# Two chained cross-attentions: where ScalarE copies a product's part and where VectorE takes the product out

## The reference

```python
# L0, per batch: x is 100 x 128, ctx is 1444 x 128
normed = x * rsqrt(mean(x**2) + 1e-6) * norm_w
q, k, v = heads(normed @ wq), heads(ctx @ wk), heads(ctx @ wv)
attn = softmax(einsum('bhqd,bhkd->bhqk', q, k))
x1 = x + merge(einsum('bhqk,bhkd->bhqd', attn, v)) @ wo
# L1
w = softmax(einsum('brd,bfd->brf', x1, ctx))
out = x1 + einsum('brf,bfd->brd', w, ctx)
```

## Time and profile before

| | us |
|---|---|
| median of 3 runs | 591.34 (590.78 to 592.22) |
| profiled execution | 590.37 |
| its span, first to last instruction | 588.6 |
| TensorE busy | 567.8 |
| VectorE busy | 456.6 |
| ScalarE busy | 392.8 |
| GpSimd busy | 457.4 |

### The profile page before, as it was taken

One profiled execution on the slowest core, in us unless ns is written; L12 is line 12 of the kernel. 1 busy time (PEld: TensorE's weight loads), 2 busy tenths in 40 slices (PEclk: granted clock), 3 DMA queues, 4 the chain that ended last, 5 costly groups with the idle time before them and its releaser, 6 DMA issues.

```text
span 588.6 us, 10834 instructions
## 1 busy us (share of the span) xinstructions
PE 567.8 (96%) x3748; PEld 513.4 (87%) x3748; DVE 456.6 (78%) x642; ACT 392.8 (67%) x515; POOL 457.4 (78%) x532
## 2 busy tenths in 40 slices
PE   7799999899999999999999999999999999999997
PEld 7678889799999899898989899998999888988885
DVE  4667789779886898868987798868987798868505
ACT  5567676857766677757767586757768486756802
POOL 3317895997879897998879987998779987998810
PEclk9889999999999999999999999999999999999999
DMA  7056847677566776676566666676676775766400
GB/s 223 1 127 152 219 122 181 162 188 167 146 168 171 199 175 162 163 193 164 145 180 179 182 172 154 185 190 156 144 184 160 209 177 146 185 148 176 119 1 9
DMA packets 47809, 92.45 MB, mean 157 GB/s; under 512 B 14699, under 2 KB 20235, under 8 KB 47755
## 3 DMA queue, kind: packets, MB, share of 16 engines
q1 hardware_dynamic: 39834, 76.71, 51.6%
q10 hardware_dynamic: 7920, 15.05, 9.6%
HBM read 8.72 MB, written 0.41 MB: 16 GB/s over the span
## 4 chain that ended last, share of the span: by engine, by line
PE 70%; DVE 9%; POOL 6%; ACT 5%; issue 4%; SPq 3%; DMA 1%; ACTq 0%; DVEq 0%; POOLq 0%
PE ps_o L1229 30%; PE ps_s L1108 10%; PE ps_s L1112 10%; PE ps_s L1109 9%; DVE neg_max L908 5%; POOL turned_p L566 4%; PE ps_m L1152 4%; PE ps_m L1013 3%; SPq L469 3%; ACT probs L711 2%; PE ps_o L1225 2%; PE ps_m L1032 1%; POOL c_lo L571 1%; DVE o_norm L882 1%; DMA x_rows<-in_x_dram 1%
## 5 line engine op out<-in xcount | busy, mean ns | idle before, releaser
L566 POOL TENSOR_TENSOR turned_p<-turned_p 128x1408 fp32r<-128x1408 f32 (+1 forms) x109 | 339.1, 3111 | 9.6 <-ACT turned_p L740 6.7
L1229 PE MATMUL ps_o<-turned_p,c_hi 128*128 128x256 f32 (+2 forms) x1273 | 248.9, 291 | 1.7 <-DVE o_norm L882 1.7
L711 ACT ACTIVATE probs<-ps_s,neg_max 128x1444 f32<-128x1444 f32 (+1 forms) x109 | 160.1, 1469 | 132.9 <-DVE neg_max L908 131.3
L908 DVE TENSOR_REDUCE neg_max<-ps_s 128x1 f32<-128x1444 f32 (+1 forms) x111 | 184.2, 1659 | 67.2 <-PE ps_s L1112 66.6
L1229 PEld LDWEIGHTS ps_o<-turned_p,c_hi 128*128 128x128 f32 x1273 | 206.4, 189 | 3.8 <-issue 3.1
L1229 PE MATMUL ps_o<-turned_p,c_lo 128*128 128x256 f32 (+2 forms) x693 | 185.5, 270 | 0.0
L931 DVE STREAM_TRANSPOSE blocks<-probs 128x1408 f32<-128x1408 f32 (+1 forms) x109 | 178.1, 1634 | 2.4 <-DMA turned_p<-blocks 1.8
L740 ACT ACTIVATE turned_p<-turned_p 128x1536 fp32r<-128x1536 f32 (+1 forms) x109 | 156.3, 1435 | 4.6 <-DMA turned_p<-blocks 4.6
L1229 PEld LDWEIGHTS ps_o<-turned_p,c_lo 128*128 128x128 f32 x693 | 131.3, 189 | 0.0
L1108 PE MATMUL ps_s<-cT_hi,q_hi 128*128 128x512 f32 (+3 forms) x312 | 122.6, 393 | 1.6 <-DVE q_lo L809 1.6
L1112 PE MATMUL ps_s<-cT_hi,q_lo 128*128 128x512 f32 (+3 forms) x312 | 119.9, 384 | 0.0
(11 more groups left out here) (147 smaller groups left out, 444.0 us busy)
## 6 DMA issues: line engine op xcount, KB each, us to landing
turned_p<-blocks SPq DMA_DIRECT2D x667, 96.0 KB, 2.3
turned_p<-blocks ACTq DMA_DIRECT2D x141, 96.0 KB, 2.7
ctx_raw<-in_ctx_dram SPq DMA_DIRECT2D x8, 704.0 KB
turned_p<-blocks SPq DMA_DIRECT2D x40, 48.0 KB, 2.0
turned_p<-blocks ACTq DMA_DIRECT2D x24, 48.0 KB, 2.1
wq_sb<-in_L_xattn_wq_dram SPq DMA_DIRECT2D x2, 256.0 KB, 5.3
wk_sb<-in_L_xattn_wk_dram SPq DMA_DIRECT2D x2, 256.0 KB, 5.5
wv_sb<-in_L_xattn_wv_dram SPq DMA_DIRECT2D x1, 512.0 KB, 6.5
```

The source lines that it names most:

```text
L566: pool.tensor_tensor(lo, lo.bitcast(F32), hi.bitcast(F32), ALU.subtract).then_inc(remainder, 1)
L711: act.activation(probs[step % 2][0:m, 0:S], score_tile(step, m), ACT.Exp, bias=neg_max[0:m, s:s + 1], accum_out=sums[0:m, s:s + 1]).then_i ...
L908: dve.tensor_reduce(neg_max[0:m, s:s + 1], score_tile(step, m), AX.X, ALU.max, negate=True).then_inc(maxed, 1)
L1229: t = pe.matmul(*todo[i], start=(i == 0), stop=(i == len(todo) - 1))
```

## The change

ScalarE: in a step that ends a unit and has an ordinary tile (not one of the three tiles that TensorE transposes at the run's end, BY_PE), copy_part(unit) is issued ahead of exponential(step), not behind it. In other steps its place is as before. VectorE: turn_blocks gets the unit and issues take_out(unit) between the main turn and the tail's turn; where there is no turn to make, it issues the take-out alone. No instruction is added or taken away, and no semaphore's value changes.

```diff
+                unit = finished_at(step + 1)
+                if unit is not None and item_at(step) is not None and step not in BY_PE:
+                    copy_part(unit)
                 exponential(step)
-                unit = finished_at(step + 1)
-                if unit is not None:
+                if unit is not None and (item_at(step) is None or step in BY_PE):
                     copy_part(unit)
                 round_bank(step, "B")
...
-            def turn_blocks(step):
+            def turn_blocks(step, unit):
+
                 item = item_at(step)
                 if item is None or step in BY_PE:
+                    if unit is not None:
+                        take_out(unit)
                     return
...
                     .then_inc(block_turned, 1)
+                if unit is not None:
+                    take_out(unit)
                 dve.wait_ge(tail_split, upto(step))
                 dve.transpose(dst[:, :, FULL * QD:RUN], tails[step % 2][0:m, :].rearrange("p (k n) -> p k n", k=4))\
...
                     invert(step - 1)
-                elif step:
-                    turn_blocks(step - 1)
                 unit = finished_at(step + 1)
-                if unit is not None:
-                    take_out(unit)
+                if step:
+                    turn_blocks(step - 1, unit)
                 read_bank(step, "B")
```

## The result

The changed kernel takes 599.33 us (median of 6 runs, 597.87 to 600.40) where the kernel before took 591.06 us on the same chips (median of 6): slower, the ratio of the runs is 1.0165 with a 95% interval of 1.0133 to 1.0196. The forecast had the sign and the place right and the size too small: 5.5 us, where the medians differ by 8.3 us and the ratio makes it 9.8 us. The profiled execution took 599.78 us, its span is 598.0 us.

What follows compares the result with a forecast made beforehand. TensorE bounds the kernel, with GpSimd's full queue arriving together with it at step 7. Losses of 2.6 us (batches 2, 4, 6), 2.1 (3, 5) and 0.8 (0, 1, 7) sum to +5.5 us: 596.8 us, range 592.5 to 600.

Steps and rivals of the forecast that it cites:

- the point that decides: GpSimd's full queue from step 4's remainder (L566) ends together with TensorE's output projection in step 7, leaving no slack.
- Even batches: Batches 2, 4, 6: step 7's product 1.00 us later, 0.14 us kept of step 9's win; net loss 0.86 us each.
- P: End of the product that ScalarE's copy waits for; copy starts at P + 0.03, a late unit's next rounding at P + 1.63.
- Odd batches: Batches 3 and 5: step 7's product 1.37 us later, less 0.33 us won in step 1; loss 1.04 us each.
- Queued behind the waiting copy: ScalarE's queue: exponential, next rounding and its DMA issues are delayed; reciprocal and GpSimd's remainder wait for these.
- Batches 0, 1, 7: Each loses between nothing and 1.04 us; 0.8 us taken for the three together.
- The other steps with a unit: Remainders there come 0.1 to 0.7 us later, with more slack than that before the product that reads them.
- The wait on L890 in batch 1: TensorE's o_norm wait of 0.9 us before step 7, counted as won and then taken back by GpSimd's queue.
- The rule on GpSimd's spans: Skill rule calling GpSimd spans unreliable: step 6's remainder might end before 321.72, leaving slack and shrinking the loss.
- the faster one: Rival: GpSimd's queue has hidden slack or rounding follows less closely; hand-overs outside step 7 win 5.2 us, 586.1; chance 0.10.
- No change: Rival: only the reciprocal's path delays GpSimd, or its queue is partly elastic; 590 to 593 us; chance 0.12.
- The third: Rival: late tail's turn delays VectorE's maxima or DMAs, 0.5 to 1 us more in 7 batches; 600 to 604; chance 0.08.

Runs made afterwards that it cites:

- The shortened tail: From batch 2 on, GpSimd's stacking of the context's tail cut to three one-column copies: 587.84 us in the changed kernel, 589.44 us in the kernel before.
- ScalarE's half alone: Kernel before with only ScalarE's copy moved ahead of the exponential, VectorE in the old order: 598.83 us, ratio 1.0139.
- VectorE's half alone: Kernel before with only VectorE's take-out moved between the turns, ScalarE in the old order: 591.17 us, ratio 1.0006.
- masks on ScalarE alone: Kernel before with ScalarE making the two masks of GpSimd's tail stacking, GpSimd only adding one step later: 585.91 us, ratio 0.9951.
- version that beats both: Kernel before plus the new order in chosen steps only, ScalarE making GpSimd's two tail masks, L892 from PSUM: 580.83 us, second set 582.09 us.

## Why the prediction was right in sign and place, and short in size

- **The bound and the point that decides** were right: GpSimd's queue between step 4's remainder and step 7's product. The shortened tail shows it from both sides.
- **Even batches**: forecast +0.86 us, measured 0.75 to 0.78. By terms, step 3 -0.33 (measured -0.33), the product of step 7 relative to step 3 +1.33 (measured 1.2), steps 9 and 11 together -0.14 (measured -0.12). The working of the queue holds too: the late copy starts at 308.42, which is P + 0.03, and the rounding at 310.02, which is P + 1.63.
- **Odd batches**: forecast +1.04 us, measured 1.93 and 1.96. The parts that were in the sum hold, -0.32 in step 1 and 1.3 in step 7. Missing were 0.45 us in step 9 and 0.51 us in step 11. The step that failed is the sentence "Queued behind the waiting copy are the exponential, the next rounding and ScalarE's own DMA issues": round_bank(step, "B") stands there too. The forecast took the order of ScalarE's step from the code and left out its last entry, and with it the path from TensorE's bank write over L657 and L811 to TensorE's next bank write. Batches 1, 3 and 5 have it: 2.9 us, as much as the whole difference between 5.5 and 8.3 us; what else was off (0.3 us too much in the even batches, 0.4 us too little in batches 0, 1 and 7) cancels. The run with those steps in the old order got just that back in its trace.
- **Batches 0, 1, 7**: forecast 0.8 us together. Measured 0.6, 1.4 and 0.1. Batch 1 holds 0.95 us of the bank hand-over and 0.44 us in step 5, batch 0 holds 0.34 us in step 11. These two are a second step that failed: "The other steps with a unit delay the remainder by 0.1 to 0.7 us by the same formula, and have more slack than that". In both the product starts behind GpSimd's late remainder, 0.06 us after its end in batch 0, so the slack was smaller than the delay. The wait on L890 in batch 1, 0.9 us, which the forecast counted as won and taken back later, was never won: it ended with that remainder. Without the bank term the three make 1.2 us, for which 0.8 was taken.
- **The rule on GpSimd's spans** (Trainium skill, Perfetto Trace Analysis, "GPSIMD Engine Instruction") would have made the loss smaller. The trace does not agree here: in the changed kernel the product of step 7 starts 0.05 us behind the printed end of the remainder in each of batches 1 to 7, and cutting the queue of the kernel before moved that product by 0.10 us in even batches. There was no hidden slack.
- **Rivals**: the faster one fell, the waits on o_norm were won and outweighed. No change fell too, the roundings did delay the remainders. The third named the tail's turn as a cause of more; it waited (L942 6.7 us for L557 on the page, before 1.3), but ScalarE's roundings waited no longer for their data than before (3.7 us, before 4.6), and TensorE's list has no wait for a transfer of turned_p and none for an exponential before the run's end. In ScalarE's half alone the late turn does reach TensorE, through the take-out behind it. That there was more to lose was right, its mechanism was another.

## What to carry to other kernels

Before an instruction that waits is moved ahead of another, list everything that its engine issues after the two, up to the next wait, the rare entries of the loop included, and follow each to the engine that waits for it; the entry that was left out cost here as much as half the forecast. A stall of 0.3 us that is won in 20 places is worth nothing where another queue arrives at the same moment, so price the second-latest arrival at every hand-over. And if an order wins in some steps and loses in others, choose by step and relieve the engine that would be the next bound: that turned +1.65% into -1.1%.

## What the runs showed of the hardware

**Two SBUF inputs and GpSimd.** L892 (both inputs in SBUF) ended 0.08 us after GpSimd's L566 in all of batches 0 to 6 of the changed kernel, in batch 4 at 314.88 after 314.80, and took 0.82 us in the median; with one input in PSUM it took 0.225 us, though in batch 4 L566 ran over all of it. In the kernel before, batch 0's instance was already like this (0.46 us, ending 0.08 us after L566), and the others ran in 0.23 to 0.37 us where no remainder was running. So VectorE's instruction waited for the end of GpSimd's. The Trainium skill says the same (SBUF — State Buffer, section "Who interferes with whom"): a VectorE instruction with two SBUF inputs contends with a GpSimd instruction that reads SBUF, and the second to start blocks. The traces agree: of the two, L566 had started first in all seven.

**The granted clock.** The runs of the kernel before lie between 586.6 and 594.4 us (one more took 1,107 us), wider than any of the single terms. Nearly all of that spread goes with the mean granted clock of the run. Medians in us by mean clock, with the number of runs:

| mean clock | 0.999, 1.000 | 0.996, 0.997 | 0.993, 0.994 | 0.990, 0.991 | 0.987 to 0.989 |
|---|---|---|---|---|---|
| kernel before | 587.1 (11) | 588.9 (26) | 590.3 (16) | 591.9 (9) | 593.9 (5) |
| changed kernel | | | 598.3 (3) | 599.9 (2) | 600.4 (1) |
| VectorE's half alone | 588.9 (2) | 590.5 (5) | 593.1 (3) | | |
| masks on ScalarE alone | 584.8 (3) | 585.9 (4) | 587.5 (1) | | |
| version that beats both | 579.6 (4) | 581.8 (3) | | 584.6 (3) | |

Within a column the kernels can be compared. The profiles show where the clock goes: ahead of the first product TensorE ran at half (1.2 GHz) for one to three stretches in eleven of the fourteen profiles, 0.93 in the mean over the first 50 us of the kernel before. In the other three, those with the masks on ScalarE, it was at 1.00 throughout. Four profiles have such stretches inside the run as well, one is shown below. Stretches by engine busy time, then clock: the kernel before, and the version that beats both.

```profile
0.00:50.00 50.00, 42.09 (x228) 35.63 (x229) 30.77 (x48) 29.72 (x48) 16.84 (x44) 0.93 0.44 122
```

```profile
0.00:50.00 50.00, 41.99 (x243) 36.25 (x244) 33.00 (x52) 31.77 (x52) 18.91 (x45) 1.00 0.47 130
```

The masks do not do away with the loss of clock: 11 of the 18 runs of those versions had a mean clock below 0.999, of the kernel before 56 of 67. Whether they make it rarer stays open. Their gain does not hang on it, since it is there in every column.

In the kernel with L892 from PSUM the clock fell inside the run too, after TensorE had waited 1.60 us for step 7's product in batch 1, and so again in batches 2 and 3:

```profile
114.60:118.00 3.40, 1.80 (x16) 1.63 (x16) 2.07 (x3) 2.93 (x3) 3.32 (x4) 0.99 0.84 236
118.00:121.40 3.40, 3.40 (x18) 3.40 (x18) 0.36 (x2) 0.00 (x0) 3.40 (x3) 0.50 0.65 156
121.40:124.80 3.40, 3.40 (x23) 3.06 (x23) 1.27 (x1) 0.00 (x0) 3.32 (x4) 1.00 0.82 228
```

Each such stretch delayed the next product by 1.5 us. What brings one about is not shown: in the same profile waits of 1.55 to 1.59 us in batches 4 to 6 were not followed by one, and another stretch, in batch 7, came after a wait of only 0.37 us. The changed kernel waits nearly as long in the same places (1.47 us in batch 4) and kept its clock in this profile. The four runs of the kernel with L892 from PSUM took 599.6 and 601.1 us at a mean clock of 0.991, where the changed kernel took 599.8 and 600.0, and 601.3 and 604.8 us at 0.986 and 0.983. So its extra 2 us go with the clock, and at the same clock no gain shows either. Whether its longer waits lower the clock is not shown.
